# Score products of blocks 1 to 7 contract over 64 rows in two row groups, two banks to one exponential

## The reference

```python
h = _L0_tok_ref(x, emb_table, norm_weight, proj_weight)      # x (2, 1024), 128 token kinds -> h (2, 1024, 512)
h = h + _L0_attn_ref(_layernorm(h), wq, wk, wv, wo)          # causal, 32 query heads, 8 key heads, head size 16
h = h + _L0_ffn_ref(_layernorm(h), w_gate, w_up, w_down)     # 512 -> 2048 -> 512, silu(gate) * up
# attention, per query head; four query heads share one key head and one value head
att = einsum('bhqd,bhkd->bhqk', q, k) / sqrt(16)
att = softmax(where(mask, -inf, att))
y = einsum('bhqk,bhkd->bhqd', att, v)
```

## Time and profile before

| | |
|---|---|
| median of 3 runs | 724.23 |
| the profiled execution's own time | 725.0 |
| its span (first to last instruction) | 723.3 |
| PE busy / PEld busy | 692.8 (96%) / 525.0 (73%) |
| DVE / ACT / POOL busy | 413.0 / 350.1 / 294.9 |
| share of PE in the chain that ended last | 86% |
| mean granted TensorE clock | 0.983 |

### The profile page before, as it was taken

How to read it: one execution, slowest core, us unless ns; L and a number is a source line. 1 busy time by engine, 2 the same in 40 slices (tenths; PEclk the granted TensorE clock), 3 DMA queues, 4 the chain that set the end, 5 groups by cost and what they waited for, 6 DMA issues and landing times.

```text
span 723.3 us, 16202 instructions
## 1 busy us (share of the span) xinstructions
PE 692.8 (96%) x6303; PEld 525.0 (73%) x6303; DVE 413.0 (57%) x1039; ACT 350.1 (48%) x722; POOL 294.9 (41%) x398
## 2 busy tenths in 40 slices
PE   8549989999999999999999999999999999999998
PEld 4328779984898569965997479856996499847873
DVE  6867689886654556554655465554655465543320
ACT  7848378862465226730665146621664066512320
POOL 5020122232366426652465436642665346621220
PEclk9859999999999999999999999999999999999999
DMA  8968310001100120003000110012000300000000
GB/s 325 350 254 314 118 47 1 2 5 56 63 2 1 47 76 1 3 4 103 16 2 2 61 60 2 2 46 76 2 2 1 106 16 2 2 15 15 1 1 29
DMA packets 10458, 40.35 MB, mean 56 GB/s; under 512 B 1808, under 2 KB 2576, under 8 KB 8592
## 3 DMA queue, kind: packets, MB, share of 16 engines
q1 hardware_dynamic: 6912, 25.44, 9.2%
q0 software_dynamic: 3328, 13.11, 5.8%
q10 hardware_dynamic: 144, 0.79, 0.3%
HBM read 29.89 MB, written 9.44 MB: 54 GB/s over the span
## 4 chain that ended last, share of the span: by engine, by line
PE 86%; DVE 7%; ACT 3%; DMA 2%; issue 2%; SPq 0%; POOL 0%; DVEq 0%; ACTq 0%; POOLq 0%
PE banks L1082 15%; PE banks L1084 15%; PE banks L1083 15%; PE banks L1169 6%; PE banks L1171 6%; PE banks L1170 6%; PE banks L1036 4%; PE banks L1054 3%; PE banks L1025 2%; PE banks L1115 2%; PE banks L1117 2%; PE banks L1116 2%; PE banks L1060 1%; PE banks L1061 1%; PE banks L1122 1%
## 5 line engine op out<-in xcount | busy, mean ns | idle before, releaser
L1084 PE MATMUL banks<-xnT_and_h,ffn_weights 128*128 128x256 f16 x1024 | 279.0, 272 | 0.0
L1082 PE MATMUL banks<-xnT_and_h,ffn_weights 128*128 128x256 f16 x1024 | 278.8, 272 | 0.1
L1083 PE MATMUL banks<-xnT_and_h,ffn_weights 128*128 128x256 f16 x1024 | 278.9, 272 | 0.0
L371 POOL TENSOR_TENSOR gated_split<-gate_work,gated_split 128x256 f16<-128x256 f32 x128 | 86.5, 675 | 261.1 <-ACT gated_split L521 261.1
L375 POOL TENSOR_TENSOR weights_split<-weights,weights_split 128x512 f16<-128x512 f32 x96 | 111.0, 1156 | 0.0
L1082 PEld LDWEIGHTS banks<-xnT_and_h,ffn_weights 128*128 128x128 f16 x1024 | 101.0, 99 | 11.9 <-DVE xnT_and_h L874 0.6
L509 ACT ACTIVATE gate_work<-banks,scales 128x256 f32<-128x256 f32 x128 | 60.5, 472 | 100.0 <-PE banks L1084 99.8
L1084 PEld LDWEIGHTS banks<-xnT_and_h,ffn_weights 128*128 128x128 f16 x1024 | 100.0, 98 | 11.7
L1083 PEld LDWEIGHTS banks<-xnT_and_h,ffn_weights 128*128 128x128 f16 x1024 | 99.9, 98 | 11.3
L824 DVE SCALAR_TENSOR_TENSOR weights<-weights,counts_T 128x512 f32<-128x512 f32 x128 | 87.5, 683 | 13.4 <-ACT weights L517 13.3
L517 ACT ACTIVATE weights<-banks,scales 128x512 f32<-128x512 f32 x128 | 87.3, 682 | 14.5 <-PE banks L1036 14.5
(11 more groups left out here) (230 smaller groups left out, 1083.3 us busy)
## 6 DMA issues: line engine op xcount, KB each, us to landing
ffn_weights<-in_ffn_w SPq DMA_DIRECT2D x12, 1024.0 KB, 11.8
out_rows_dram<-ffn_weights SPq DMA_DIRECT2D x16, 256.0 KB, 2.0
xnT_and_h<-in_wqkv SPq DMA_DIRECT2D x1, 1536.0 KB, 8.3
local_table<-gated_split SPq DMA_DIRECT2D x2, 640.0 KB, 4.7
local_table<-xnT_and_h SPq DMA_DIRECT2D x2, 640.0 KB, 3.6
gated_split<-in_projT SPq DMA_DIRECT2D x4, 256.0 KB, 4.5
ffn_weights<-in_wo SPq DMA_DIRECT2D x1, 1024.0 KB, 10.3
token_table<-weights_split ACTq DMA_DIRECT2D x1, 768.0 KB, 8.3
```

The source lines that it names most:

```text
L371: g.tensor_tensor(gtl[:, j, :], g2[j % 2], gth[:, j, :], ALU.subtract).then_inc(gt_lo, 1)
L1082: t.matmul(o, wh, xTh[m % 2][:, c, :], start=c == 0, stop=False)
L1083: t.matmul(o, wh, xTl[m % 2][:, c, :], start=False, stop=False)
L1084: last = t.matmul(o, wl, xTh[m % 2][:, c, :], start=False, stop=c == DC - 1)
```

## The change

From unit 16 on (V >= UPB, blocks 1 to 7, 112 units), `score` takes only the 64 rows of a head: rows 0 to 63 for the even head of a pair, 64 to 127 for the odd one, in both the key table and `Qst`. The even heads write the first half of bank 4, the odd heads the first half of bank 5. One exponential reads the two halves by a pattern of two pieces of 256 columns. Every unit now uses both banks, so `score(V)` waits for the exponential of unit V - 1. The heads lie in the weights in another order (0, 2, 1, 3), which `head_block` undoes where `values` reads them. Block 0 stays as it is. The number of instructions is the same.

```diff
+        S_pair = ps[:, 4 * 512:6 * 512].rearrange("p (a x) -> p a x", a=2)[:, :, 0:2 * P]
...
+        def head_block(V, h):
+            return h if V < UPB else (h % 2) * 2 + h // 2
...
-                        a.activation(E[V % RING][:, :], b_S[V % 2], ACT.Exp, scale=c_exp).then_inc(exp_done, 1)
+                        if V < UPB:
+                            a.activation(E[V % RING][:, :], b_S[V % 2], ACT.Exp, scale=c_exp).then_inc(exp_done, 1)
+                        else:
+                            a.activation(E[V % RING][:, :].rearrange("p (a x) -> p a x", a=2), S_pair, ACT.Exp,
+                                         scale=c_exp).then_inc(exp_done, 1)
...
                 if V >= 2:
-                    pe.wait_ge(exp_done, V - 1)
+                    pe.wait_ge(exp_done, V - 1 if V < UPB else V)
                 r = V % RING
+                if V >= UPB:
+                    for j in range(2):
+                        for a in range(2):
+                            rows = slice(a * STK, (a + 1) * STK)
+                            last = t.matmul(b_S[a][:, j * P:(j + 1) * P], (KstA, KstB)[a][rows, gr * P:(gr + 1) * P],
+                                            Qst[rows, r * 256 + j * P:r * 256 + (j + 1) * P], start=True, stop=True)
+                    last.then_inc(scores, 1)
+                    return
...
-                        last = t.matmul(o, E[r][:, h * P:(h + 1) * P], Vf3[:, gr, :], start=True, stop=True)
+                        e = head_block(V, h) * P
+                        last = t.matmul(o, E[r][:, e:e + P], Vf3[:, gr, :], start=True, stop=True)
```

More of the change, by code:

```diff
@@ L1059, in values @@
                     o = b_PV[:, ((V % 2) * REP + h) * PVW:((V % 2) * REP + h + 1) * PVW]
-                    t.matmul(o, WTh[r][:, h * P:(h + 1) * P], Va3[:, gr, :], start=True, stop=False)
-                    last = t.matmul(o, WTl[r][:, h * P:(h + 1) * P], Va3[:, gr, :], start=False, stop=True)
+                    e = head_block(V, h) * P
+                    t.matmul(o, WTh[r][:, e:e + P], Va3[:, gr, :], start=True, stop=False)
+                    last = t.matmul(o, WTl[r][:, e:e + P], Va3[:, gr, :], start=False, stop=True)
                 last.then_inc(pv_rdy, 1)
```

## The result

The changed kernel takes 737.16 us (median of 4 runs, 736.77 to 738.37) against 724.25 for the kernel before in the same set (four runs); the ratio is 1.0171, with a 95% interval of 1.014 to 1.0203, so the kernel is slower. The prediction was 716.0. Here are the page's lines of the changed kernel on the busy engines and the granted clock.

What follows compares the result with a forecast made beforehand. PE was taken to bound the kernel; 106 units sparing 0.084 each, 8.9, less 0.6 for a wait in block 1, gave 8.3 less: 716.0 us by the median. The range was 712.5 to 752.

Steps and rivals of the forecast that it cites:

- The bound: Blocks 1 to 7: PE is busy 96% of the span; whatever PE is spared in a slot shortens the slot.
- Four products over half the rows: Each unit's score products: two stream at once, 0.139 instead of 0.223, sparing 0.084 a unit, 0.114 at best.
- Going from 128 rows to 64 and back: Before and after each unit's score products: taken as costing nothing, with bounds of 0 and 0.163 a change.
- rival B: A short settling at each row-count change, say 0.056, losing 0.028 a unit: 727.8 us; chance 0.12.
- Rival A: Array runs empty at each change between 64 and 128 rows, losing 0.242 a unit: 750.4 us; chance 0.25.
- Weight loads and `head_block`: Score products' loads keep their number and keep up with a 0.027 pitch; the head reordering only changes addresses: nothing.
- The exponential over two banks: Each unit's exponential reads 512 numbers a partition as before, 0.68 now; twice as long would still be covered.
- The new wait at the start of block 1: Unit 17's scores wait for unit 16's exponential and start 0.58 later; cost 0.58, once.
- Slot 15: Blocks 2 to 7: unit 15's saving is waited away in slot 16, so 6 of 112 units give nothing.
- Sum: Whole kernel: 106 x 0.084 = 8.9 spared, 0.6 added, 8.3 less; 716.0 us by the median.

Runs made afterwards that it cites:

- the run with 128 rows: Changed kernel with two banks and one exponential over both, but every score product again over all 128 rows; 726.97 us, ratio 1.0019 against the kernel before.
- the one in the other order: Changed kernel with a unit's four score products ordered even, even, odd, odd head instead of even, odd, even, odd; 738.42 us, ratio 1.0161 against the kernel before.
- the repetition: The changed kernel run once more, unaltered, to look at the start of block 1; 737.54 us, ratio 1.0171 against the kernel before.

## Why the prediction was wrong

*The bound.* Right. PE is full, and what a slot gains or loses on PE is the time.

*Four products over half the rows.* Right in mechanism, and a little better than taken. Starts at 0, 0.01, 0.07 and 0.07 instead of 0, 0.027, 0.056 and 0.083. The 27 ns of setup were an average over pairs that start together: record by record, the sixteen of that row start 3 to 4 ns apart within a pair and 52 to 63 ns apart from pair to pair. The Trainium skill ("TensorE: Matmul & The Clock Gate", Part 3, The mechanism) has about 4 ns between row groups; the traces agree, with 3 or 4 ns within a pair of the changed kernel's scores too.

*Going from 128 rows to 64 and back.* This step failed: "I take nothing, because the nearest behaviour, full-array products back to back and half-array ones back to back, is limited by streaming alone in both." The runs showed 0.10 for each change, in both directions, for rows and for columns, independent of whether a pair runs at once (22.0, 45.1 and 23.9 for 2, 4 and 2 changes a unit). It was between the ends that I had given, 0 and 0.163, above the 0.056 of rival B, and well above the 0.042 at which the sign turns. In place of 0.084 spared, a unit lost 0.10. The bounds were right; the choice of the end was not. Products that follow each other in one shape say nothing on what lies between two shapes, and the earlier trace rows, with every change behind a wait, should have been read as a lack of evidence and not as its nearest row.

The Trainium skill ("TensorEngine Tiling (Array Packing)", Key Properties) had said that changing the tiling mode drains TensorE. The traces agree that a change isn't free, with 0.10 as the price; that it is a drain isn't shown. What the rows show is that the next shape's weights are not loaded ahead, and that load and product both start about 0.10 later than the pitch would have it, however wide the product before: 0.31 against 0.216 after 512 columns (slot 0 of block 4 in the changed kernel, the rows below), 0.20 against 0.109 after 256, 0.15 to 0.16 against 0.056 after 128. In all three the next shape starts 0.07 before the modelled end of the product before (348.61 against 348.68 in the rows below, 351.66 against 351.73 and 351.88 against 351.95 in those of unit 65). Rival A waited for that end, and this is by how much its 0.163 was too high.

```profile
348.30 0.38 PE L1190 MATMUL banks<-ffn_weights,gated_split 128*128 128x512 f16 x1
348.61 0.23 PE L1047 MATMUL banks<-q_stack,k_stack_even 64*128 64x128 f16 x1
```

*Weight loads and `head_block`.* As forecast, nothing by themselves within the four products; at a change, the load starts no earlier than the product. *The exponential over two banks.* Nothing: 0.68 as before; the run with 128 rows has it and is unchanged after unit 17.

*The new wait at the start of block 1.* 0.58 forecast, 0.66 between the units, 0.6 in the run without the row groups. The difference is that the scores start 0.15 after the exponential's end (98.50 + 0.68 to 99.33), where 0.06 was taken. What I left out is the clock: the longer gap stands next to another of 0.48, and in two of four profiled executions with that wait (the changed kernel's first, and the one in the other order) the clock then fell to its lower level; in the other two it did not. Each had the same two gaps, 1.65 from the end of one to the end of the other.

*Slot 15.* Right: it changed nothing in blocks 2 to 7; what was waited away there was a loss and not the forecast gain.

*Sum.* 106 x 0.10 + 0.6 = 11.2, and with the fall of the clock, 1.7, it is 12.9; measured 12.8 from unit 16 on in the profiled execution. The medians' 12.9 is no finer proof, since in the repetition they lie 12.1 apart, and in how many executions the clock fell isn't known. The range held the time, because rivals A and B were in it; the forecast's direction was wrong.

## What to carry to other kernels

Using a part of the array pays only if many products stay in that shape. Here the way in and out costs 0.20 together and a pair at once spares 0.056 over two in turn: four products lost 0.10, eight were 0.01 to 0.02 ahead, so by these numbers (products of 128 columns, 64 rows) a trip breaks even at seven to eight. The one version with such trips was slower as a whole, for the wait that its moved transposes brought. Zero rows that keep all products in one shape are the cheaper form of a small contraction between full ones. When a trace has a resource in two modes but never one right behind the other, take the change between them as unknown, and test it with one instruction before building on it.

## What the runs showed of the hardware

- A change of the array's shape costs about 0.10 us at full clock, for 64 of 128 rows (after products of 128, 256 and 512 columns) and for 64 of 128 columns (into them after 256, and back).
- Products of different row groups don't keep the program's order by their records: in the order even, even, odd, odd the third starts before the second. The Trainium skill ("TensorE: Matmul & The Clock Gate", Part 3, The mechanism) has matmuls start and end in program order; the records of this run have the starts otherwise, by 0.06. The ends of records are modelled, so nothing is said of them.
- The granted clock fell from its 2.4 GHz to its 1.2 GHz level behind idle gaps of 0.48 and 1.14 whose ends are 1.65 apart, in two profiled executions and not in two others. The fall cost 1.7. What decides it stayed open.
- Not tried: more than two units in one trip, for which there are no banks free, and a trip in which other products than scores use half the array too.
